# A decoder layer on one core: a new order for the start and the loop of its mixture of experts

## The chip, the core and the metric

The kernel runs on one core of a Trainium2 chip. A core has five engines that take instructions from queues of their own and meet only at semaphores: TensorE (PE in the profile, with PEld for its weight loads), VectorE (DVE), ScalarE (ACT), GpSimd (POOL) and SyncE (SP), which here only issues DMAs. Every queue is worked off in the order in which it was written; an instruction that waits holds up all that stand behind it on its engine.

The metric is the device time of one execution in microseconds (us), on one core. The changed kernel is compared with the kernel before by that.

## The reference

One decoder layer on x of 4 x 256 tokens by 256 features: 16 gated heads (projection, causal convolution, layer norm, a decaying state), an attention over a context, and a mixture of experts. The change is in the last, and where it begins:

```python
scores = sigmoid(hidden @ gate_weight.T)                  # 1024 tokens x 16 experts
choice = scores + bias                                    # 4 groups of 4 experts
# sum of the two best of each group -> keep 2 groups -> keep the 4 best experts of them
topk_weight = 2.5 * topk_weight / (topk_weight.sum(-1) + 1e-20)
g = einsum('th,nfh->ntf', hidden, gate_w)                 # 16 experts, 128 wide
u = einsum('th,nfh->ntf', hidden, up_w)
act = silu(g) * u
routed = einsum('ntf,nhf,tn->th', act, down_w, weight_matrix)
out = routed + swiglu(hidden, sh_gate_w, sh_up_w, sh_down_w)   # one shared expert, 256 wide
x = x + out
```

## The kernel before, in words

The program has three stages: the 16 heads in a software pipeline (up to about 400 us), a middle stage (last projection, layer norm, context attention, layer norm; about 400 to 430 us), and the experts. No scheduler places anything: each engine's order is the order of the code of its block, and semaphore counts tie the engines together.

The shared expert is cut into two of 128, so there are 18 experts, n = 1 to 18, of which 1 and 2 are the shared ones. The 1024 tokens are worked in NCH = 2 chunks c of N = 512. Each fp32 product is made of three fp32r products of a high and a low part (`mm3`, L1250 to L1254: low-high, high-low, high-high), so every matrix is first split: ACT copies the high part, POOL or DVE subtracts to get the low one. For one expert:

- SP loads its three weight matrices, 384 KB, into one half `s` of `w_raw` (`load_expert`, DMA L356).
- ACT and POOL split the two matrices of the first products (`gate_up_high` L759, `gate_up_low` L482) and that of the second (`down_high` L766, `down_low` L488) into the same half of `w_hi` and `w_lo`.
- PE makes g and u of each chunk into four banks, 24 matmuls of 512 columns (`gate_up`).
- ACT takes silu(g) (`gate_silu`, `tok`, L775), DVE multiplies by u (`u_times`, `conv`, L1142), POOL multiplies by the routing weights (`weigh`, `gate<-conv,tap`, L500), ACT and DVE split the product (`act_high` L784, `act_low` L1151, tiles `gated_hi` and `gated_lo`).
- PE makes the second product, 24 matmuls of 256 columns, added up in banks 4 to 7 (`down`).

Below, G(n) is `gate_up` of expert n on PE and D(n) its `down`. PE goes G(n+1), D(n). Buffers for silu, product and split product are single.

The routing weights of an expert are a row of `route_rows` in DRAM. SP loads it, spread over 128 partitions, 512 KB, into one half of `tap0` (`load_route`, DMA L378); `weigh(n)` waits for it. For experts 1 and 2 the weight is 1, made by a memset on POOL (L506). The rows come out of the routing chain: PE makes the logits (L1252 to L1254 with `wv_hi`), ACT the sigmoid, PE transposes to tokens (L1613), ACT copies (L804), DVE runs some 40 small dependent operations (L1171 to L1231), PE transposes back (L1628), ACT copies to `routeT` (L816), SP writes `route_rows` (L372). While that chain runs, the engines work on experts 1 to 3 in between.

Of the kernel before, what the change touches and what calls it, by code (L numbers as in the profile page):

```python
# [25 lines left out]
P = 128  # L26
# [4 lines left out]
N = 512  # L31
# [95 lines left out]
def decoder_layer(nc, x_in, ctx_in, xw_in, xb_in, wb_in, bb_in, w_in, prm_in, wv_in, wo_in,  # L127
# [5 lines left out]
    with ctx:  # L133
# [75 lines left out]
        act_w = gate  # L209
        act_hi, act_lo = gated_hi[:, 0:T], gated_lo[:, 0:T]  # L210
        wb_hi, wb_lo = act_hi[:, 0:KT * H], act_lo[:, 0:KT * H]

# [45 lines left out]
        ones_ready = sem("ones_ready")  # L258
# [9 lines left out]
        def _(sp):  # L268
# [90 lines left out]
            def expert_split(n):  # L359


                sp.wait_ge(down_lo_ready, n - E_SHARED)


# [5 lines left out]
            load_expert(4, 1)  # L370
            sp.wait_ge(r_tr_ready, NCH)
# [3 lines left out]
            def load_route(e, s, before):  # L375

                sp.wait_ge(e_weighted, before)
                sp.dma_start(wbc[:, s * T:(s + 1) * T],  # L378
                             route_rows[bass.ds(e, 1), :].broadcast_to([P, T])).then_inc(ld_route[s], 16)

            for s in range(2):
                load_route(s, s, NCH * (s + 1))
# [12 lines left out]
        def _(pool):  # L395
# [89 lines left out]
            def down_low(n, s):  # L485
                w = slice(s * 3 * D + 2 * D, (s + 1) * 3 * D)
                pool.wait_ge(down_hi_ready, n - E_SHARED)
# [3 lines left out]
            def weigh(n, s, first):  # L491

                for c in range(NCH):
                    pool.wait_ge(u_prod, (n - 1) * NCH + c + 1)
                    if not first:

                        pool.wait_ge(e_hi, (n - 2) * NCH + c + 1)
                        pool.wait_ge(e_lo, (n - 2) * NCH + c + 1)
                    cc = slice(c * N, (c + 1) * N)
                    nc.gpsimd.tensor_tensor(act_w[:, cc], prod[:, cc], wbc[:, s * T + c * N:s * T + (c + 1) * N],  # L500
                                            ALU.mult).then_inc(e_weighted, 1)
# [12 lines left out]
            def step(n, s, left=2):  # L514

                pool.wait_ge(ld_route[s], (n - 1 - s) * 8)
                weigh(n, s, False)
                if left > 1:
                    gate_up_low(n + 2, s)
                if left > 0:  # L520
                    down_low(n + 1, 1 - s)

            with pool.Fori(0, E_ROUTED // 2 - 1) as r:
                for s in range(2):
                    step(r * 2 + (3 + s), s)
            step(E_ALL - 1, 0, 1)
            step(E_ALL, 1, 0)
# [3 lines left out]
        def _(act):  # L531
# [220 lines left out]

            def gate_up_high(n, s):
# [3 lines left out]
                act.wait_ge(e_full, n * 4 - 8)  # L757
# [3 lines left out]
            def down_high(n, s):  # L761
                act.wait_ge(ld_w[s], n * 8 + (8 * (H - 1 - s) + 16))
# [5 lines left out]
            def gate_silu(n, first):  # L768

                for c in range(NCH):  # L770
                    act.wait_ge(e_full, (n - 1) * 4 + 2 * c + 1)
                    if not first:
                        act.wait_ge(u_prod, (n - 2) * NCH + c + 1)
                    cc = slice(c * N, (c + 1) * N)
                    nc.scalar.activation(silu_g[:, cc], e_ring[2 * c][:, :], ACT.Silu).then_inc(g_silu, 1)  # L775

            def act_high(n, first):

                for c in range(NCH):
                    act.wait_ge(e_weighted, (n - 1) * NCH + c + 1)  # L780
                    if not first:
                        act.wait_ge(e_down, n - 1)
                    cc = slice(c * N, (c + 1) * N)
                    nc.scalar.activation(act_hi[:, cc], act_w[:, cc], ACT.Copy).then_inc(e_hi, 1)  # L784
# [5 lines left out]
            context_soft(1)  # L790
            context_att()
# [5 lines left out]
            for c in range(NCH):  # L797

# [3 lines left out]

            act.wait_ge(r_tok_full, 1)
            nc.scalar.activation(score, bank[4][:, 0:TT * E_ROUTED], ACT.Copy).then_inc(r_tok_ready, 1)  # L804
            gate_silu(1, True)
            gate_up_high(3, 0)
            act_high(1, True)
            gate_silu(2, False)
            gate_up_high(4, 1)
            act_high(2, False)  # L810
            down_high(3, 0)

# [6 lines left out]
            def step(n, s, left=2):  # L819
                gate_silu(n, False)  # L820
                if left > 1:
                    gate_up_high(n + 2, s)
                act_high(n, False)
                if left > 0:
                    down_high(n + 1, 1 - s)

            with act.Fori(0, E_ROUTED // 2 - 1) as r:
                for s in range(2):
                    step(r * 2 + (3 + s), s)
# [872 lines left out]
```

## Time and profile before

| | us |
|---|---|
| median of 3 runs (lowest, highest) | 597.23 (596.89, 598.12) |
| the profiled execution's own time | 597.47 |
| its span in the profile | 595.7 |
| PE busy | 558.7 (94% of the span) |
| DVE busy | 433.7 (73%) |
| ACT busy | 399.5 (67%) |
| POOL busy | 299.0 (50%) |

The busy times are sums over the span; matmuls overlap by design, so a PE that is busy 10.00 of 10 us is one without a gap, and the distance between the starts of two matmuls is what one costs. The profile names a tile by what its buffer was first made for: in the experts' stage `tok` is silu(g), `conv` the product with u, `gate` the weighted product, `gated_hi` and `gated_lo` its two parts, `obet` and `raw` the routing's tiles, `tap` the weights of one expert.

### The profile page before, as it was taken

How to read it: one execution, taken by the hardware profiler on the slowest of the kernel's cores; microseconds unless marked ns; L12 is line 12 of the kernel's file. 1: busy time of each engine (PE TensorE's matmuls, PEld its weight loads, DVE VectorE, ACT ScalarE, POOL GpSimd, SP SyncE). 2: the span in 40 equal slices, each digit the busy share in tenths (PEclk: the TensorE clock that was granted, in tenths of full speed). 3: DMA queues.
4: the chain of work that ended last, by engine and by line, in shares of the span. 5: the costliest groups of instructions: out<-in, count | busy, mean ns of one | idle time of the engine just before them, and what ended most of it. 6: DMA issues, size and time to landing. Idle time of an engine off the chain costs nothing.

```text
span 595.7 us, 10301 instructions
## 1 busy us (share of the span) xinstructions
PE 558.7 (94%) x3392; PEld 490.0 (82%) x3392; DVE 433.7 (73%) x1018; ACT 399.5 (67%) x783; POOL 299.0 (50%) x201
## 2 busy tenths in 40 slices
PE   3899999999999999999999999896687999999996
PEld 1687899989989989989989989786475888888885
DVE  8778989889989988998998998955676433333334
ACT  4978988878978979879779778674442433344331
POOL 2434756746746646656656563301032755556542
PEclk9998999999999999999999999998797999999999
DMA  6122032032032032032031020110001523333311
GB/s 202 41 99 81 0 117 81 1 115 81 2 117 81 2 115 81 2 116 80 2 116 55 28 97 27 55 30 0 1 1 51 172 101 110 102 123 115 105 62 70
DMA packets 16267, 42.23 MB, mean 71 GB/s; under 512 B 4544, under 2 KB 4800, under 8 KB 16224
## 3 DMA queue, kind: packets, MB, share of 16 engines
q1 hardware_dynamic: 16224, 41.69, 21.1%
q8 instruction: 23, 0.38, 0.3%
q14 instruction: 20, 0.16, 0.1%
HBM read 40.47 MB, written 1.21 MB: 70 GB/s over the span
## 4 chain that ended last, share of the span: by engine, by line
PE 84%; DVE 8%; ACT 5%; issue 1%; DMA 1%; SPq 0%; DVEq 0%; ACTq 0%
PE bank L1252 20%; PE bank L1254 19%; PE bank L1253 19%; PE bank L1248 15%; PE bank L1386 4%; PE bank L1374 4%; ACT tok L622 2%; PE bank L1263 1%; DMA xbias<-in_xb 1%; DVE stats L969 1%; ACT values L536 1%; DVE stats L889 1%; DVE x L1242 0%; DVE raw L988 0%; DVE conv L1142 0%
## 5 line engine op out<-in xcount | busy, mean ns | idle before, releaser
L1252 PE MATMUL bank<-xT_lo,w_hi 128*128 128x512 f32 x336 | 140.7, 419 | 2.3 <-DVE conv L988 1.2
L1254 PE MATMUL bank<-xT_hi,w_hi 128*128 128x512 f32 x336 | 132.6, 395 | 0.0
L1253 PE MATMUL bank<-xT_hi,w_lo 128*128 128x512 f32 x336 | 132.4, 394 | 0.0
L423 POOL TENSOR_TENSOR gated_lo<-gated,gated_hi 128x512 fp32r<-128x512 f32 x30 | 38.7, 1289 | 116.5 <-ACT gated_hi L642 112.8
L622 ACT ACTIVATE tok<-bank,nmr,rstd 128x128 f32<-128x128 f32 x256 | 91.2, 504 | 2.1 <-DVE nmr L884 2.1
L500 POOL TENSOR_TENSOR gate<-conv,tap 128x512 f32<-128x512 f32 x36 | 46.5, 1293 | 86.7 <-DVE conv L1142 76.0
L1252 PEld LDWEIGHTS bank<-xT_lo,w_hi 128*128 128x128 f32 x336 | 63.9, 190 | 17.4 <-DVE conv L988 3.2
L1254 PEld LDWEIGHTS bank<-xT_hi,w_hi 128*128 128x128 f32 x336 | 63.6, 189 | 14.4
L418 POOL TENSOR_TENSOR conv<-tap,conv 128x506 f32<-128x506 f32 x32 | 61.9, 1934 | 21.7 <-DVE conv L988 21.7
L418 POOL TENSOR_TENSOR raw<-tap,raw 128x506 f32<-128x506 f32 x32 | 62.0, 1936 | 20.4 <-DVE raw L988 16.3
L1253 PEld LDWEIGHTS bank<-xT_hi,w_lo 128*128 128x128 f32 x336 | 64.1, 191 | 9.7
L969 DVE BATCH_NORM_STATS2 stats<-bank 128x6 f32<-128x128 f32 x256 | 56.4, 284 | 16.1 <-PE bank L1374 16.1
L960 DVE TENSOR_TENSOR_SCAN decay<-obet,dmask 128x1536 f32<-128x1536 f32 x16 | 62.0, 3872 | 0.0
L1142 DVE TENSOR_TENSOR conv<-bank,tok 128x512 f32<-128x512 f32 x36 | 24.9, 691 | 46.1 <-PE bank L1254 43.8
L1151 DVE TENSOR_TENSOR gated_lo<-gate,gated_hi 128x512 fp32r<-128x512 f32 x36 | 25.4, 746 | 44.1 <-ACT gated_hi L784 44.1
L634 ACT ACTIVATE qk<-bank,prm 128x512 f32<-128x512 f32 x64 | 51.3, 841 | 0.0
L988 DVE SCALAR_TENSOR_TENSOR raw<-bank,prm,raw 128x510 f32<-128x510 f32 x64 | 46.8, 743 | 5.6 <-ACT tap L590 4.5
L1248 PE MATMUL bank<-qk 128*128 128x256 f32 (+1 forms) x256 | 50.2, 329 | 0.5 <-DVE x L1021 0.3
L988 DVE SCALAR_TENSOR_TENSOR conv<-bank,prm,conv 128x510 f32<-128x510 f32 x64 | 46.8, 743 | 3.4 <-ACT tap L590 2.2
L1248 PEld LDWEIGHTS bank<-qk 128*128 128x128 f32 x256 | 43.2, 190 | 5.6 <-issue 0.7
L1248 PE MATMUL bank<-probs,values 128*128 128x256 f32 (+1 forms) x256 | 46.9, 327 | 0.0
L784 ACT ACTIVATE gated_hi<-gate 128x512 fp32r<-128x512 f32 x36 | 21.0, 625 | 37.6 <-PE bank L1254 32.4
(167 smaller groups left out, 1374.3 us busy)
## 6 DMA issues: line engine op xcount, KB each, us to landing
w_raw<-in_w SPq DMA_DIRECT2D x34, 384.0 KB, 4.4
obet<-obet_rows SPq DMA_DIRECT2D x16, 768.0 KB, 4.3
tap<-route_rows SPq DMA_DIRECT2D x16, 512.0 KB, 3.6
wv_raw<-in_wv SPq DMA_DIRECT2D x8, 256.0 KB, 4.9
wo_raw<-in_wo SPq DMA_DIRECT2D x8, 256.0 KB, 5.0
x<-in_x SPq DMA_DIRECT2D x2, 512.0 KB, 4.7
out_x<-x SPq DMA_DIRECT2D x4, 256.0 KB, 2.4
raw<-in_ctx SPq DMA_DIRECT2D x1, 512.0 KB, 5.4
```

The source lines that it names most:

```text
L418: nc.gpsimd.tensor_tensor(y, r, y, ALU.add).then_inc(conv_done, 1)
L423: nc.gpsimd.tensor_tensor(gated_lo[:, cc], gated[:, c * N:(c + 1) * N], gated_hi[:, cc].bitcast(F32), ALU.subtract).then_inc(gated_lo_read ...
L500: nc.gpsimd.tensor_tensor(act_w[:, cc], prod[:, cc], wbc[:, s * T + c * N:s * T + (c + 1) * N], ALU.mult).then_inc(e_weighted, 1)
L622: ins = nc.scalar.activation(tok[:, t * P:(t + 1) * P], t_ring[u][:, i * P:(i + 1) * P], ACT.Identity, scale=rstd[:, t:t + 1], bias=nmr[:, ...
L634: nc.scalar.activation(qk[:, u * N:(u + 1) * N], t_ring[u][:, :], ACT.Identity, scale=prm[:, o:o + 1], bias=prm[:, o + 1:o + 2]).then_inc( ...
L960: nc.vector.tensor_tensor_scan(decay[:, :], obet[:, :], dmask[:, :], 0.0, ALU.mult, ALU.add).then_inc(decay_ready, 1)
L969: ins = nc.vector.bn_stats(stats[:, 6 * t:6 * t + 6], t_ring[u][:, i * P:(i + 1) * P])
L988: ins = nc.vector.scalar_tensor_tensor(out=y, in0=r, scalar=prm[:, o + 3 - back:o + 4 - back], in1=y, op0=ALU.mult, op1=ALU.add)
L1248: return nc.tensor.matmul(o, l, r, start=start, stop=stop)
L1252: nc.tensor.matmul(o, l_hi, r_lo, start=start, stop=False, skip_group_check=loose)
L1253: nc.tensor.matmul(o, l_lo, r_hi, start=False, stop=False, skip_group_check=loose)
L1254: return nc.tensor.matmul(o, l_hi, r_hi, start=False, stop=stop, skip_group_check=loose)
```

## The change

The middle stage keeps its order but for two pieces put into it. From there on:

- PE's loop goes G(n), D(n-2) in place of G(n), D(n-1): the first products are two experts ahead. Silu, product, weighted product and its two parts get two buffers each.
- Experts 3 and 4 are split as a whole in the middle stage, into `wv_hi`/`wv_lo` and `wo_hi`/`wo_lo`, which the heads have left (`early_high` on ACT, one piece before `context_att`; `early_low` on POOL after the first addition of `x`). SP loads experts 5 and 6 at once behind them.
- POOL does nothing between that and the end of the routing chain: experts 1 and 2 are no longer weighed, their product is split directly, the memset is gone, and the splits of 5 and 6 wait for `r_ready`.
- In the routing chain DVE takes the first product of expert 1 before it and `act_low` of expert 2 into it; PE transposes to tokens after one bank of G(1) in place of two, and makes all of G(3) and half of D(2) before it waits for the routing weights, where it made half of G(3).
- In the loop POOL goes `weigh` of chunk 0, `gate_up_low(n+1)`, `weigh` of chunk 1, `down_low(n)`. SP goes `load_route(n)`, wait for `down_low(n)`, `load_expert(n+2)`.

The diff at its core:

```diff
@@ sync
+            for n in (5, 6):
+                sp.wait_ge(w_lo_ready, n - 2 + H)
+                load_expert(n, 1 - n % 2)
...
-            def load_route(e, s, before):
-                sp.wait_ge(e_weighted, before)
+            def load_route(e, s):
+                if not (isinstance(e, int) and e < 2):
+                    sp.wait_ge(e_weighted, e * NCH - NCH)
...
-            with sp.Fori(0, E_ROUTED // 2 - 1) as r:
+            with sp.Fori(0, E_ROUTED // 2 - 2) as r:
                 for s in range(2):
-                    expert_split(r * 2 + (3 + s))
-                    load_expert(r * 2 + (5 + s), s)
-                    load_route(r * 2 + (2 + s), s, r * (2 * NCH) + NCH * (3 + s))
+                    load_route(r * 2 + (2 + s), s)
+                    sp.wait_ge(down_lo_ready, r * 2 + (s + 1))
+                    load_expert(r * 2 + (7 + s), s)
+            for s in range(2):
+                load_route(E_ROUTED - 2 + s, s)
@@ gpsimd
-            pool.wait_ge(p_added, TT // 2)
-            nc.gpsimd.memset(wbc, 1.0).then_inc(ones_ready, 1)
-            pool.wait_ge(ones_ready, 1)
-            weigh(1, 0, True)
-            gate_up_low(3, 0)
-            weigh(2, 1, False)
-            gate_up_low(4, 1)
-            down_low(3, 0)
+            pool.wait_ge(x_mixed, 1)
+            early_low(3)
+            early_low(4)
+            pool.wait_ge(r_ready, 1)
+            gate_up_low(5, 0)
+            gate_up_low(6, 1)
...
+            def step(n, m, s, up=True, down=True):
+                pool.wait_ge(ld_route[s], n * 8 - (1 + s) * 8)
+                weigh(n, m, s, 0)
+                if up:
+                    gate_up_low(n + 1, 1 - s)
+                weigh(n, m, s, 1)
+                if down:
+                    down_low(n, s)
@@ scalar
+            def step(n, m, s, up=True):
+                gate_silu(n, m)
+                if up:
+                    gate_up_high(n + 1, 1 - s)
+                act_high(n, m)
+                down_high(n, s)
@@ vector
+            u_times(1, 1, (0,))
             dve.wait_ge(r_tok_ready, 1)
...
-            u_times(1, True, (0,))
...
-            act_low(1)
-            u_times(2, chunks=(0,))
+            u_times(2, 2, (0,))
+            act_low(1, 1)
...
+            act_low(2, 2)
             op(nc.vector.tensor_tensor(weight, same, score, ALU.mult))
@@ tensor
-            gate_up(1, 0, True, (0,))
+            gate_up(1, 0, ((0, 0),))
...
-            down(1, 0, True, False)
-            gate_up(3, 0, chunks=(0,))
+            down(1, 1, 0)
+            gate_up(3, 0)
+            down(2, 2, 1, (0,))
             pe.wait_ge(r_ready, 1)
...
-            with pe.Fori(0, E_ROUTED // 2 - 1) as r:
+            with pe.Fori(0, E_ROUTED // 2 - 2) as r:
                 for s in range(2):
-                    gate_up(r * 2 + (5 + s), s)
-                    down(r * 2 + (4 + s), 1 - s, False, False)
-            down(E_ALL, 1, False, True)
+                    gate_up(r * 2 + (7 + s), s)
+                    down(r * 2 + (5 + s), 5 + s, s)
+            down(E_ALL - 1, E_ALL - 1, 0)
+            down(E_ALL, E_ALL, 1)
```

SyncE from the write of `route_rows` through its loop, in the kernel before (`tap0` is the routing weights of one expert, L356 the load of an expert's weights):

```order
L372 DMA route_rows<-gate 16x1024 [waits r_tr_ready]
L378 DMA tap0<-route_rows 128x1024 [waits e_weighted,ld_route_rows]
L378 DMA tap0<-route_rows 128x1024 [waits e_weighted]
...
L356 ISA [waits down_lo_ready]
L356 DMA w_raw<-in_w 128x768
...
L378 ISA [waits e_weighted]
L378 DMA tap0<-route_rows 128x1024
```

The same place now (L390 loads the routing weights, L370 an expert's weights):

```order
L390 DMA tap0<-route_rows 128x1024 [waits ld_route_rows]
L390 DMA tap0<-route_rows 128x1024
...
L390 ISA [waits e_weighted]
L390 DMA tap0<-route_rows 128x1024
...
L370 ISA [waits down_lo_ready]
L370 DMA w_raw<-in_w 128x768
...
L390 ISA [waits e_weighted]
L390 DMA tap0<-route_rows 128x1024
```

In both, the load of a row of routing weights stands behind a load of expert weights and that load's wait for a `down_low`. Before, the row of expert n stood behind `down_low(n-2)`; now it stands behind `down_low(n-1)`.

GpSimd in one half of its loop, in the kernel before:

```order
L494 ISA [waits ld_route1]
L500 TENSOR_TENSOR gate<-conv,tap0 128x512 [waits e_lo,e_hi,u_prod]
...
L500 TENSOR_TENSOR gate<-conv,tap0 128x512 [waits e_lo,e_hi,u_prod]
...
L482 TENSOR_TENSOR w_lo<-w_raw,w_hi 128x512 [waits w_hi_ready]
L488 TENSOR_TENSOR w_lo<-w_raw,w_hi 128x256 [waits down_hi_ready]
```

And now:

```order
L515 ISA [waits ld_route1]
...
L520 TENSOR_TENSOR gate<-conv,tap0 128x512 [waits e_lo,e_hi]
...
L497 TENSOR_TENSOR w_lo<-w_raw,w_hi 128x512 [waits w_hi_ready]
...
L520 TENSOR_TENSOR gate<-conv,tap0 128x512 [waits e_lo,e_hi]
...
L503 TENSOR_TENSOR w_lo<-w_raw,w_hi 128x256 [waits down_hi_ready]
```

The split of the next first weights moved between the two weighings; the split of the down weights, which before was that of expert n+1, is now that of expert n and stands behind both.

## Rows read from the trace of the kernel before

**Rows 1.** Windows: stretch, length, busy us of the five, PEclk, DMA share, GB/s.

```profile
440.00:450.00 10.00, 8.46 (x49) 6.93 (x47) 9.72 (x23) 2.92 (x6) 5.27 (x5) 1.00 0.00 0
450.00:460.00 10.00, 5.81 (x20) 3.99 (x19) 5.19 (x11) 3.03 (x6) 1.76 (x2) 0.66 0.10 29
460.00:480.00 20.00, 20.00 (x124) 17.98 (x123) 8.05 (x9) 6.95 (x13) 12.51 (x11) 1.00 0.46 154
```

**Rows 2.** Timeline of PE in routing: start, us, instruction, [idle before <- its releaser].

```profile
444.30 0.36 PE L1252 MATMUL bank<-w_lo,gated_hi 128*128 128x256 f32 x1 [1.54 <-DVE gated_lo L1151]
...
453.59 1.88 PE L1628 MATMUL bank<-ident,obet 128*16 128x128 f32 x8 [3.52 <-DVE obet L1231]
456.14 0.79 PE L1252 MATMUL bank<-xT_lo,w_hi 128*128 128x512 f32 x1 [0.68 <-ACT gate L816]
...
460.46 0.28 PE L1252 MATMUL bank<-w_lo,gated_hi 128*128 128x256 f32 x1
```

**Rows 3.** Timeline of DVE in the routing chain.

```profile
434.68 0.29 DVE L1171 TENSOR_TENSOR obet<-obet 128x128 f32<-128x128 f32 x1 [5.28 <-ACT obet L804]
...
437.82 1.27 DVE L1195 TENSOR_TENSOR raw<-raw,tie 128x128 f32<-128x128 f32 x1
439.13 0.29 DVE L1196 TENSOR_TENSOR raw<-raw 128x128 f32<-128x128 f32 x1
...
443.46 1.29 DVE L1151 TENSOR_TENSOR gated_lo<-gate,gated_hi 128x512 fp32r<-128x512 f32 x2
...
451.22 0.69 DVE L1223 TENSOR_TENSOR raw<-raw 128x128 f32<-128x128 f32 x1
```

**Rows 4.** Timeline of POOL in the same stretch.

```profile
437.53 1.41 POOL L500 TENSOR_TENSOR gate<-conv,tap 128x512 f32<-128x512 f32 x1 [32.82 <-DVE conv L1142]
...
462.47 2.54 POOL L500 TENSOR_TENSOR gate<-conv,tap 128x512 f32<-128x512 f32 x2 [10.71 <-DMA tap<-route_rows]
```

**Rows 5.** Timeline of SP: its DMA issues.

```profile
458.05 0.81 SPq L378 DMA_DIRECT2D tap<-route_rows  x2
459.22 0.35 SPq L356 DMA_DIRECT2D w_raw<-in_w  x1
...
482.79 0.33 SPq L356 DMA_DIRECT2D w_raw<-in_w  x1
```

**Rows 6.** DMA issues from 450 us, KB, median to landing; under it L378's spread.

```profile
w_raw<-in_w SPq DMA_DIRECT2D x14, 384.0 KB, 3.0
...
DMA to landing us min/median/max: 3.3/3.6/5.0
```

**Rows 7.** POOL in the loop; the last row gives min/median/max ns of L488.

```profile
468.84 2.54 POOL L500 TENSOR_TENSOR gate<-conv,tap 128x512 f32<-128x512 f32 x2 [1.23 <-DVE conv L1142]
...
481.60 1.02 POOL L488 TENSOR_TENSOR w_lo<-w_raw,w_hi 128x256 fp32r<-128x256 f32 x1 [0.77 <-ACT w_hi L766]
...
L488 POOL TENSOR_TENSOR w_lo<-w_raw,w_hi x16: 748/1016/1088, 451.0 to 580.9; 128x256 fp32r<-128x256 f32 x16
```

**Rows 8.** Timeline of ACT late in the loop.

```profile
579.35 1.16 ACT L784 ACTIVATE gated_hi<-gate 128x512 fp32r<-128x512 f32 x2 [3.63 <-PE bank L1254]
580.41 0.40 ACT L766 ACTIVATE w_hi<-w_raw 128x256 fp32r<-128x256 f32 x1
```

**Rows 9.** Timeline of PE: starts of G(5), D(4), G(6); then the end of the stage.

```profile
471.53 0.40 PE L1252 MATMUL bank<-xT_lo,w_hi 128*128 128x512 f32 x1
...
477.01 0.28 PE L1252 MATMUL bank<-w_lo,gated_hi 128*128 128x256 f32 x1
...
479.81 0.40 PE L1252 MATMUL bank<-xT_lo,w_hi 128*128 128x512 f32 x1
...
589.12 0.36 PE L1252 MATMUL bank<-w_lo,gated_hi 128*128 128x256 f32 x1 [1.59 <-DVE gated_lo L1151]
...
591.88 0.27 PE L1254 MATMUL bank<-w_hi,gated_hi 128*128 128x256 f32 x1
```

**Rows 10.** Timeline of ACT in the middle stage, behind `context_att`.

```profile
406.68 2.07 ACT L536 ACTIVATE values<-x,nmr,rstd 128x256 f32<-128x256 f32 x4 [2.37 <-DVE nmr L884]
```

More of the change, by code:

```diff
@@ L486, in down_low @@
                 w = slice(s * 3 * D + 2 * D, (s + 1) * 3 * D)
-                pool.wait_ge(down_hi_ready, n - E_SHARED)
+                pool.wait_ge(down_hi_ready, n - 4)
                 nc.gpsimd.tensor_tensor(w_lo[:, w], w_raw[:, w], w_hi[:, w].bitcast(F32),
                                         ALU.subtract).then_inc(down_lo_ready, 1)
[L491 to L501, printed above, removed]
@@ L523, in _, with early_low, weigh @@
-            with pool.Fori(0, E_ROUTED // 2 - 1) as r:
+            def early_low(n):
+                hi, lo = early(n)
+                s = 1 - n % 2
+                pool.wait_ge(w_hi_ready, n + H)
+                nc.gpsimd.tensor_tensor(lo, w_raw[:, s * 3 * D:(s + 1) * 3 * D], hi.bitcast(F32),
+                                        ALU.subtract).then_inc(w_lo_ready, 1)
+            def weigh(n, m, s, c):
+                pool.wait_ge(u_prod, n * NCH + (c + 1 - NCH))
+                if not (isinstance(n, int) and n < 5):
+                    pool.wait_ge(e_hi, n * NCH + (c + 1 - 3 * NCH))
+                    pool.wait_ge(e_lo, n * NCH + (c + 1 - 3 * NCH))
+                nc.gpsimd.tensor_tensor(weighted(m, c), prod[:, two(m, c)],
+                                        wbc[:, s * T + c * N:s * T + (c + 1) * N],
+                                        ALU.mult).then_inc(e_weighted, 1)
@@ L766, in down_high, with gate_silu, act_high @@
                 nc.scalar.activation(w_hi[:, w], w_raw[:, w], ACT.Copy).then_inc(down_hi_ready, 1)
[L768 to L784, printed above, removed]
+            def gate_silu(n, m, chunks=range(NCH)):
+                for c in chunks:
+                    act.wait_ge(e_full, n * 4 + (2 * c - 3))
+                    if not (isinstance(n, int) and n < 3):
+                        act.wait_ge(u_prod, n * NCH + (c + 1 - 3 * NCH))
+                    nc.scalar.activation(silu_g[:, two(m, c)], e_ring[2 * c][:, :], ACT.Silu).then_inc(g_silu, 1)
+            def act_high(n, m, chunks=range(NCH)):
+                for c in chunks:
+                    if m <= E_SHARED:
+                        act.wait_ge(u_prod, (n - 1) * NCH + c + 1)
+                    else:
+                        act.wait_ge(e_weighted, n * NCH + (c + 1 - 3 * NCH))
+                        act.wait_ge(e_down, n - 2)
+                    nc.scalar.activation(act_hi[:, two(m, c)], weighted(m, c), ACT.Copy).then_inc(e_hi, 1)
             act.wait_ge(ld["router"], 32)
@@ L790, in _ @@
             context_soft(1)
+            early_high(3)
+            early_high(4)
             context_att()
@@ L796, in _, with router_scores @@
                     half_out(i, c, dst)
-            for c in range(NCH):
+            def router_scores(c):
                 act.wait_ge(r_full, c + 1)
@@ L817, in _ @@
                                      ACT.Copy).then_inc(r_tr_ready, 1)
[L819 to L827, printed above, removed]
+            def step(n, m, s, up=True):
[4 more added lines that the diff above has]
+                down_high(n, s)
+            gate_silu(4, 4)
+            act_high(3, 3)
+            gate_silu(5, 5)
+            act_high(4, 4)
+            act_high(5, 5)
+            down_high(5, 0)
+            step(6, 6, 1)
+            with act.Fori(0, E_ROUTED // 2 - 3) as r:
                 for s in range(2):
-                    step(r * 2 + (3 + s), s)
-            step(E_ALL - 1, 0, 1)
-            step(E_ALL, 1, 0)
+                    step(r * 2 + (7 + s), 7 + s, s)
+            step(E_ALL - 1, E_ALL - 1, 0)
+            step(E_ALL, E_ALL, 1, False)
         @block.vector
@@ L1587, in down @@
[L1587 to L1602 removed]
+                hi, lo = w_hi[:, s * 3 * D:(s + 1) * 3 * D], w_lo[:, s * 3 * D:(s + 1) * 3 * D]
@@ new lines, in gate_up @@
+                if isinstance(n, int) and n in (3, 4):
+                    hi, lo = early(n)
+                for c, j in parts:
+                    if not (isinstance(n, int) and n == 1):
+                        pe.wait_ge(g_silu if j == 0 else u_prod, n * NCH + (c + 1 - 2 * NCH))
+                    for kt in range(KT):
+                        o = j * D + kt * P
+                        ins = mm3(e_ring[2 * c + j][:, :], hi[:, o:o + P], lo[:, o:o + P],
+                                  xs_(xT_hi, kt, c * N, (c + 1) * N), xs_(xT_lo, kt, c * N, (c + 1) * N),
+                                  kt == 0, kt == KT - 1)
+                    ins.then_inc(e_full, 1)
```

170 lines of the change are left out of this document (97 added, 73 removed).

## The prediction, made before the changed kernel ran

> **What bounds the kernel now.** I read the windows first, to see where PE has gaps. From 460 us on PE is busy 20.00 of 20 us at full clock; between 440 and 460 it is busy 8.46 and 5.81 of 10 [rows 1]. So the experts' loop is bound by PE itself, and only its start has something to give. The timeline of PE gives the loop's beat: G(5) starts at 471.53, D(4) at 477.01, G(6) at 479.81, so a G is 5.48, a D 2.80, together 8.28 us [rows 9]. At that beat no other engine's order can make the loop faster, but a chain longer than 8.28 us per expert can make it slower. The gaps are these: 1.54 us before D(1), 3.52 before the routing transposes, 0.68 before the second half of G(3), and 1.59 before D(18) [rows 2, 9]. Then the timeline of DVE, since the 3.52 end with its chain, and those of SP and POOL, since their order in the loop is what the change turns.
>
> **What the start gains.** The clock: with the 3.52 us gap the mean granted clock of 450 to 460 is 0.66, and with the 1.54 gap that of 440 to 450 stays 1.00 [rows 1, 2]. The second half of G(3) takes 4.32 us (456.14 to 460.46) against 2.74 at full clock, the eight transposes 1.88 [rows 2], of which I take half, 0.94, as clock.
>
> DVE's chain runs from 434.68 to 453.5 without a pause [rows 2, 3]. Seven of its small operations, from the first at 437.82 (1.27 us) to the last at 451.22 (0.69), lie beside a POOL instruction such as that of 437.53 and cost 7.8 us, where the same shape takes 0.29 [rows 3, 4]: some 5.9 us. With POOL idle they go. The chain starts 0.4 later (first product of expert 1 ahead of it), loses 0.8 (that product and a wait inside it) and gets `act_low(2)`, 1.2 net of overlap [rows 3]. It ends at 453.5 + 0.4 - 5.9 - 0.8 + 1.2 = 448.4. By then PE has G(3) and half of D(2) ahead of it: G(2) ends at 442.6, and D(1) needs `act_low(1)`, which now stands behind no weighing and is due at about 442.0. So D(1) runs to 445.4, G(3) to 450.9, half of D(2) to 452.3, and the transposes find the weights ready. All three gaps and the low clock go: 1.54 + 3.52 + 0.68 + 1.58 + 0.94 = 8.3 us. G(4) starts at 455.0, not 463.3 (460.46 + 2.80). At the end D(17) and D(18) both follow G(18), and 1.6 us goes too. With the old beat in between that would be 9.9 us.
>
> **What the middle stage pays.** Two ACT copies before `context_att`: behind it ACT waits 2.37 us for the norm [rows 10], and two copies of 768 columns are shorter than that, with 0.53 for 512 [rows 8]. I take 0. Two subtractions on POOL beside DVE's additions and statistics of `x`: no row shows these beside a POOL instruction that reads SBUF. Bounds: 0, and 1.0 for one DVE operation held as at 437.82 [rows 3]; I take 0, since DVE waits there for PE's sums one after the other and has room. The Trainium skill, page "SBUF — State Buffer", section "SBUF: two separate sides", says that DVE and GpSimd exclude each other only where DVE has two SBUF inputs or a two-port mode. By it the statistics (one input) and the additions (one input in PSUM) go free; the rows of the routing chain, all from SBUF, agree with its other half.
>
> **What the loop pays.** This decides. In SP's queue the load of row n stands behind the load of expert n+1, which waits for `down_low(n-1)`. POOL's step n begins with `weigh(n)`, which waits for row n, and ends with `down_low(n)`. So POOL waits for SP, and SP for POOL's last instruction, one full turn per expert with a whole DMA in it. The buffer has been free for long; the place in the queue alone makes the chain. One turn:
>
> - `down_low(n-1)` ends to SP's issue: 481.60 + 1.02 to 482.79, 0.17 [rows 5, 7].
> - The load of expert n+1 is issued ahead: 0.45, from two issues in 0.81 [rows 5].
> - Row n lands. Alone 3.3 to 5.0, median 3.6; the 5.0 had another row's load right in front [rows 6]. Here 384 KB stand in front, alone 3.0 [rows 6]. In the one burst of the trace (two rows and an expert from 458.05) POOL had its first row at 462.47, after 4.4 [rows 4, 5]. I take 4.3; bounds 3.6 and 5.0. Then 0.05 to POOL.
> - Three POOL operations (weigh, low part of the next first weights, weigh) by 2.54 for two: 3.8 [rows 7]. The low part's source has landed before the row.
> - `act_high` of chunk 1 and `down_high` on ACT, 0.53 + 0.40 and hand-overs: 1.03 [rows 8].
> - `down_low(n)`: 1.02, the median; bounds 0.75 and 1.09 [rows 7].
> - POOL's second weighing beside DVE's `act_low` of chunk 0: 0 to 0.34 (1.09 - 0.75) [rows 7], I take 0.17; and 0.1 for SP's loop branch every second turn, an estimate, bounds 0 and 0.2.
>
> Sum: 0.17 + 0.45 + 4.35 + 3.8 + 1.03 + 1.02 + 0.27 = 11.1 us, against PE's 8.28. Low bound 9.8, high 12.1. G(n+1) waits for its low part, the second of the three POOL operations, so PE takes this beat and stands idle 2.8 us before each G.
>
> The Trainium skill, page "DMA: Bandwidth & Descriptors", section "Anatomy of one DMA", gives about 2.0 us fixed plus bytes at 436 GB/s for a DMA issued from GpSimd. Put here, as an estimate, 896 KB would land 4.1 us after the first issue, so 3.65 after the row's, and a turn would be 10.4. This trace is above it: 3.0 for 384 KB, where it gives 2.9, and 3.6 for a row, where it gives 3.2.
>
> Where the turns begin: PE has made its transposes at 453.2 (with ACT's copies about 454.1). From ACT's copy to the first weighing it was 6.33 us (456.14 to 462.47) [rows 2, 4], so `weigh(3)` starts at 460.4 and ends at 462.9. Row 5 is issued then and lands at 466.8 (3.6 + 0.2, nothing before it). `weigh(5)`, ACT and `down_low(5)` take 2.54 + 1.03 + 1.02: 471.4. Then expert 7 and row 6: 0.17 + 0.45 + 4.35, 476.35. G(7) starts two POOL operations later, 478.95. PE has done G(4) to G(6), D(3), D(4) by 455.0 + 16.4 + 5.6 = 477.0 and waits 1.9. From G(7) to G(18) are 11 turns: 478.95 + 122.1 = 601.05. After G(18) stand D(16), D(17), D(18), with the work of expert 18 (some 4 us) under the first two: 5.48 + 8.40 + 0.16 for the last matmul's end = 14.04, so 615.1. The old kernel's PE ended at 592.15 and its span at 595.7: 3.55 more [rows 9]. Span 618.6. The profiled execution is 1.77 above its span and 0.24 above the median of the runs, so the time is 618.6 + 1.77 - 0.24 = 620.2 us, 23 slower.
>
> **The rivals.**
>
> *The loop stays at PE's beat.* Then the 9.9 us are won: 587.3. For it: PE has a lead of two experts, and before POOL's wait for the first row [rows 4] was its only one on a row. Against: a lead of any length is used up by a turn that is longer than the beat, and for a turn of 8.28 row n would have to land 1.5 us after its issue; the fastest took 3.3 [rows 6]. It needs that I read the queue wrongly. 5%.
>
> *Cheaper turns.* The row lands as if alone, 3.6, and nothing collides: 9.8, so 11 x 1.3 = 14.3 less, 606. 15%.
>
> *Dearer turns.* Row at 5.0 and collisions: 12.1, 631. 12%.
>
> *The clock falls in the waits.* A wait of 2.8 lies between the 1.54 that cost nothing and the 3.52 that did [rows 1, 2]. G would be slower by 1.6 per half at the low clock [rows 2]. Up to 2.8 a turn this hides in PE's wait, since POOL's turn doesn't see it; only after the last wait it counts: 2 to 3 us, 623, inside my range. PE could become the bound at up to (5.48 + 2.80) x 2 only if the clock never came back, and in every busy stretch it did. 10% for a cost that shows.
>
> **How the numbers follow.** The forecast, turns near 11, has 58%, the rivals 5, 15, 12 and 10. All but the first are slower. A measurement of this kernel tells 0.2% (1.2 us) from no change. Faster 5%, same 1%, slower 94%. The range of 8 in 10 goes from 608 to 630; it leaves out the first rival and the outer halves of the two on the turns.
>
> **What would show it.** Right: PE waits 2 to 3 us before each G from G(7) on, released by POOL's low part; the largest wait of POOL is on the load of `tap`, about 4.5 us each, 12 or 13 times; each `tap` issue lies 0.4 to 0.5 behind a `w_raw` issue; G starts 10 to 12 us apart; the routing stage without its gaps, G(4) starting near 455, DVE's small operations all near 0.3. Wrong: `tap` issued well before `down_low`, or G's 8.28 apart. If the turns are right and the total isn't, the start's 8.3 is the term to look at.

## The result, and the profile after

The kernel after takes 630.69 us (median of 4 runs, 626.80 to 633.84) against 597.06 us (596.17 to 598.12) for the kernel before on the same chip: a ratio of 1.0559, 95% interval 1.0489 to 1.0630. The prediction was 620.2 us, with a range of 608 to 630. The kernel is slower, as forecast, and in the place that was forecast, but its time lies 10.5 us above the forecast and 0.7 us above the upper end of the range. The profiled execution took 628.59 us, its span is 626.6.

The windows show both halves of the change. Columns are as in [rows 1]: the stretch, its length, busy us of PE, PEld, DVE, ACT and POOL, granted clock, DMA share, GB/s.

```profile
440.00:450.00 10.00, 10.00 (x61) 8.78 (x60) 7.44 (x28) 3.38 (x6) 0.98 (x1) 1.00 0.00 0
450.00:460.00 10.00, 10.00 (x57) 8.48 (x56) 1.38 (x2) 2.26 (x4) 1.73 (x3) 1.00 0.33 106
460.00:470.00 10.00, 10.00 (x58) 8.74 (x57) 7.69 (x8) 4.86 (x9) 9.06 (x6) 1.00 0.16 60
470.00:480.00 10.00, 6.47 (x37) 5.67 (x36) 3.10 (x4) 2.57 (x5) 4.97 (x4) 0.88 0.28 93
480.00:500.00 20.00, 18.45 (x94) 15.59 (x92) 5.15 (x7) 5.94 (x11) 6.21 (x6) 0.89 0.28 93
500.00:600.00 100.00, 75.94 (x392) 64.68 (x393) 26.85 (x34) 28.44 (x52) 45.19 (x36) 0.93 0.22 73
```

PE is busy 10.00 of 10 us through the whole routing stage, where it was busy 8.46 and 5.81 [rows 1]. Then, from 470 us, it has gaps: in the loop it is busy 75.94 of 100 us, where it had none (80.00 of 80 us from 500 to 580 in the kernel before).

The routing chain on DVE has become what was forecast. The shape that took 1.27 us beside GpSimd [rows 3] takes 0.28 to 0.29 in the whole chain (`L1244` is the old L1195):

```profile
435.55 0.29 DVE L1244 TENSOR_TENSOR raw<-raw,tie 128x128 f32<-128x128 f32 x1
...
446.27 0.29 DVE L1281 TENSOR_TENSOR obet<-obet 128x128 f32<-128x128 f32 x1
```

The loss stands in the timeline of SyncE. First comes each expert's weights, then the row of routing weights, and both wait for the last instruction of GpSimd's step:

```profile
506.73 0.33 SPq L370 DMA_DIRECT2D w_raw<-in_w  x1
507.63 0.33 SPq L390 DMA_DIRECT2D tap<-route_rows  x1
519.07 0.33 SPq L370 DMA_DIRECT2D w_raw<-in_w  x1
519.69 0.33 SPq L390 DMA_DIRECT2D tap<-route_rows  x1
```

And in the timeline of POOL beside it (the bracket is the idle time before, and what ended it):

```profile
505.62 0.94 POOL L503 TENSOR_TENSOR w_lo<-w_raw,w_hi 128x256 fp32r<-128x256 f32 x1 [1.05 <-ACT w_hi L803]
512.75 1.26 POOL L520 TENSOR_TENSOR gate<-conv,tap 128x512 f32<-128x512 f32 x1 [6.19 <-DMA tap<-route_rows]
513.97 1.26 POOL L497 TENSOR_TENSOR w_lo<-w_raw,w_hi 128x512 fp32r<-128x512 f32 x1
515.19 1.72 POOL L520 TENSOR_TENSOR gate<-conv,tap 128x512 f32<-128x512 f32 x1
517.96 0.93 POOL L503 TENSOR_TENSOR w_lo<-w_raw,w_hi 128x256 fp32r<-128x256 f32 x1 [1.05 <-ACT w_hi L803]
```

Read one turn through both: `down_low` ends at 506.56, the weights are issued at 506.73, the row at 507.63; the row releases the weighing at 512.75; `down_low` ends at 518.89, and the next issue is at 519.07. That is 12.3 us for an expert, and a load is in it from issue to landing. The timeline of PE shows that it takes this turn as its own (start of G(7), G(8), G(9), G(10), then G(18)):

```profile
478.60 0.79 PE L1309 MATMUL bank<-xT_lo,w_hi 128*128 128x512 f32 x1 [3.52 <-POOL w_lo L497]
...
491.44 0.49 PE L1309 MATMUL bank<-xT_lo,w_hi 128*128 128x512 f32 x1 [1.54 <-POOL w_lo L497]
...
503.01 0.49 PE L1309 MATMUL bank<-xT_lo,w_hi 128*128 128x512 f32 x1 [3.01 <-POOL w_lo L497]
...
515.37 0.79 PE L1309 MATMUL bank<-xT_lo,w_hi 128*128 128x512 f32 x1 [3.83 <-POOL w_lo L497]
...
608.73 0.49 PE L1309 MATMUL bank<-xT_lo,w_hi 128*128 128x512 f32 x1 [1.67 <-POOL w_lo L497]
```

From 478.60 to 608.73 there are 11 turns of 11.83 us, against PE's 8.28 before [rows 9]. The waits from 455 us on, summed (engine, line, releaser: us, times, longest), name the same chain: GpSimd waits for the row, ScalarE for GpSimd, and PE for the low part of its weights:

```profile
POOL gate L520 <- DMA tap<-route_rows: 71.1, 13, 8.3
ACT gated_hi L821 <- POOL gate L520: 64.0, 27, 3.5
...
PE bank L1309 <- POOL w_lo L497: 30.8, 12, 3.8
```

### The profile page after: what moved, and what is told of

The parts are those of the page before. It is cut to its first block, busy times and chain, and to the rows that moved or that the text cites. A ratio compares the mean times of both kernels' runs of the same rounds, so it can differ in the third digit from the quotient of the medians.

```text
span 626.6 us, 10166 instructions
## 1 busy us (share of the span) xinstructions
PE 567.1 (91%) x3392; PEld 495.0 (79%) x3392; DVE 434.0 (69%) x1018; ACT 400.5 (64%) x781; POOL 295.9 (47%) x194
## 4 chain that ended last, share of the span: by engine, by line
PE 64%; issue 8%; POOL 8%; DMA 7%; DVE 5%; ACT 5%; SPq 1%; POOLq 0%; DVEq 0%; ACTq 0%
PE bank L1305 14%; PE bank L1309 14%; PE bank L1311 13%; PE bank L1310 13%; DMA tap<-route_rows 7%; PE bank L1443 4%; PE bank L1431 4%; POOL gate L520 4%; POOL w_lo L497 3%; ACT tok L645 2%; POOL w_lo L503 1%; PE bank L1320 1%; DMA w_raw<-in_w 1%; DVE stats L1017 1%; ACT values L559 1%
## 5 line engine op out<-in xcount | busy, mean ns | idle before, releaser
L1309 PE MATMUL bank<-xT_lo,w_hi 128*128 128x512 f32 x320 | 138.2, 432 | 32.4 <-POOL w_lo L497 30.8
L1311 PE MATMUL bank<-xT_hi,w_hi 128*128 128x512 f32 x320 | 128.9, 403 | 0.0
L1310 PE MATMUL bank<-xT_hi,w_lo 128*128 128x512 f32 x320 | 128.3, 401 | 0.0
L1309 PEld LDWEIGHTS bank<-xT_lo,w_hi 128*128 128x128 f32 x320 | 62.5, 195 | 49.3 <-issue 33.1
L1200 DVE TENSOR_TENSOR gated_lo<-gate,gated_hi 128x512 fp32r<-128x512 f32 x32 | 29.5, 925 | 74.5 <-ACT gated_hi L821 74.5
L1311 PEld LDWEIGHTS bank<-xT_hi,w_hi 128*128 128x128 f32 x320 | 62.0, 194 | 14.4
L1310 PEld LDWEIGHTS bank<-xT_hi,w_lo 128*128 128x128 f32 x320 | 62.8, 196 | 9.9
```

The lines of the kernel that those rows point to most:

```text
L1309: nc.tensor.matmul(o, l_hi, r_lo, start=start, stop=False, skip_group_check=loose)
L1310: nc.tensor.matmul(o, l_lo, r_hi, start=False, stop=False, skip_group_check=loose)
L1311: return nc.tensor.matmul(o, l_hi, r_hi, start=False, stop=stop, skip_group_check=loose)
```

## The experiments

The theory: the place of the row's load in SyncE's queue makes a serial turn of SyncE, DMA, GpSimd and ScalarE, and nothing else of the change costs time. The rivals: the new order of GpSimd's step costs it, or the new order of PE, or the weights' landing. And within the theory one question was open, since the prediction's turn was too short: what makes the row's landing long. Nine kernels were run; each ratio is to the kernel before on the same chip, with its 95% interval.

### The row early

Only SyncE changes: the load of a row stands one expert earlier, ahead of the wait for `down_low`.

```diff
-            for s in range(2):
-                load_route(s, s)
+            for s in range(4):
+                load_route(s, s % 2)
             with sp.Fori(0, E_ROUTED // 2 - 2) as r:
                 for s in range(2):
-                    load_route(r * 2 + (2 + s), s)
+                    load_route(r * 2 + (4 + s), s)
                     sp.wait_ge(down_lo_ready, r * 2 + (s + 1))
                     load_expert(r * 2 + (7 + s), s)
-            for s in range(2):
-                load_route(E_ROUTED - 2 + s, s)
```

> The changed kernel with one edit in SyncE's order: the row of routing weights of expert n is loaded ahead of the wait for down_low(n-2), and no longer behind down_low(n-1). All DMAs and all other queues stay. Theory A (the turn POOL - SP - row - POOL sets the loop): the turn is cut, since the row is issued a whole step before it is needed; PE takes its own beat of 8.28 us again, no waits before G(7) to G(18), time about 587 us, ratio to the kernel before 0.983. Rival B (the load of the expert's weights, which still stands behind down_low, is what the loop waits for): POOL no longer waits for tap, but PE still waits before each G, starts of G 11 to 12 us apart, time over 620. In between: the weights' own turn (end of D(n-2), act_high, down_high, down_low, DMA 3.0, gate_up_high, gate_up_low) is 7.9 us by the rows of before against 8.28; should it be a little over, 0.5 us a step, about 593.

Measured: 596.86 us (594.99 to 599.32), ratio 0.9997 (0.9981 to 1.0014). The place of one load is worth 34 us, so the turn is shown. But it came out 10 us above what I expected: the gains of the start are there, and something in the loop eats them. The timeline of POOL (here L495 is the low part of the next first weights):

```profile
494.02 1.29 POOL L518 TENSOR_TENSOR gate<-conv,tap 128x512 f32<-128x512 f32 x1 [1.28 <-DVE conv L1190]
497.18 1.29 POOL L495 TENSOR_TENSOR w_lo<-w_raw,w_hi 128x512 fp32r<-128x512 f32 x1 [1.87 <-ACT w_hi L795]
...
500.77 0.93 POOL L501 TENSOR_TENSOR w_lo<-w_raw,w_hi 128x256 fp32r<-128x256 f32 x1 [1.05 <-ACT w_hi L801]
502.78 1.29 POOL L518 TENSOR_TENSOR gate<-conv,tap 128x512 f32<-128x512 f32 x1 [1.08 <-DVE conv L1190]
506.17 1.28 POOL L495 TENSOR_TENSOR w_lo<-w_raw,w_hi 128x512 fp32r<-128x512 f32 x1 [2.10 <-ACT w_hi L795]
```

No weighing of the loop waits for a row any more (the two such waits that are left, 8.7 us, stand ahead of it). From 497.18 to 506.17 is a second turn, 8.99 us: the low part of expert n+1, the second weighing, ACT, `down_low(n)`, and only then SyncE may load the weights of n+2 (issued at 501.88), whose high part GpSimd then awaits. It too is longer than 8.28, by 0.7 us. From G(7) to G(18) a turn is 9.04 us in the mean, 8.4 us more in 11 turns than at PE's beat, and PE waits another 2.04 us before G(7).

### The row behind `down_low`, but ahead of the weights

```diff
                     sp.wait_ge(down_lo_ready, r * 2 + (s + 1))
+                    load_route(r * 2 + (3 + s), 1 - s)
                     load_expert(r * 2 + (7 + s), s)
```

> The changed kernel, where row n is still issued only behind down_low(n-1), but ahead of the load of expert n+1's weights and not behind it. The turn stays closed, the row has nothing in front. Theory A: the turn loses the 0.74 us between the two issues and the row lands in 3.5 and not 4.7: 11.75 - 0.74 - 1.2 = 9.8 us a turn, 11 turns, about 21 us less than the changed kernel: 609. Rival B (weights): now the weights land later, so the time is the same or up to 5 us longer, 630 to 635.

Measured: 618.12 us (617.62 to 618.49), ratio 1.0351 (1.0332 to 1.0370). The turn is 10.86 (row issues from 480.74 to 589.29, ten turns). It lost the spacing of the two issues, but the row, from its issue to the weighing, became shorter only from 4.70 to 4.27 us, not to 3.5, with nothing in front of it and 384 KB 0.52 us behind it:

```profile
480.74 0.33 SPq L390 DMA_DIRECT2D tap<-route_rows  x1
481.26 0.33 SPq L370 DMA_DIRECT2D w_raw<-in_w  x1
```

### GpSimd's order turned back

```diff
                 weigh(n, m, s, 0)
+                weigh(n, m, s, 1)
                 if up:
                     gate_up_low(n + 1, 1 - s)
-                weigh(n, m, s, 1)
```

> The changed kernel with only POOL's order in a step turned: both weighings, then gate_up_low(n+1), then down_low(n). The same instructions. Theory A: gate_up_low (1.25 us) fills POOL's wait of 1.05 for ACT's act_high and down_high, so a turn is about 1.0 us shorter: 10.7, 11 turns, 11 less, about 619, though each G now starts behind three POOL operations and not two. Rival B: G waits for gate_up_low, which now comes 1.3 us later in every step, so the time is longer, 640 to 645.

Measured: 626.96 us (622.71 to 628.25), ratio 1.0509 (1.0482 to 1.0536): 3.7 us better than the kernel after, though the executions of the two overlap (622.71 to 628.25 and 626.80 to 633.84). So the new order of GpSimd is no main cause, and turning it back is not worth the 11 us that theory A gave it. The turn is 11.1 us in the mean (issues of weights from 470.59 to 592.76, eleven turns). ACT's 1 us hides beside the low part in some turns, but in others a weighing waits for its product, since G of that expert started a GpSimd operation later:

```profile
510.16 1.30 POOL L520 TENSOR_TENSOR gate<-conv,tap 128x512 f32<-128x512 f32 x1 [6.10 <-DMA tap<-route_rows]
512.60 1.29 POOL L520 TENSOR_TENSOR gate<-conv,tap 128x512 f32<-128x512 f32 x1 [1.14 <-DVE conv L1192]
```

### PE one ahead again, the row early

The kernel of the first experiment, and PE's loop back to G(n), D(n-1).

```diff
+            down(5, 5, 0)
...
                     gate_up(r * 2 + (7 + s), s)
-                    down(r * 2 + (5 + s), 5 + s, s)
-            down(E_ALL - 1, E_ALL - 1, 0)
+                    down(r * 2 + (6 + s), 6 + s, 1 - s)
             down(E_ALL, E_ALL, 1)
```

> The edit of e1_row_early, and PE's loop back to G(n), D(n-1), with D(4) and D(5) behind G(6); the rest of the change stays. It prices the first products two ahead once the rows come in time. If PE is the bound in both, this differs only at the end, by the gap before D(18) of 1.6 us: 588.6. If the two-ahead order itself is what is short of time for the weights in e1_row_early, this one is faster than that.

Measured: 601.99 us (599.84 to 602.61), ratio 1.0074 (1.0046 to 1.0101), 5 us slower than with two ahead. So PE's new order costs nothing; it wins.

### The weights in two loads

The row early, and an expert's weights in two DMAs: the 256 KB of the first product as soon as their half has been split, the 128 KB of the second behind `down_low`. That takes the second turn away as well.

```diff
+            def load_up(n, s):
+                sp.wait_ge(w_lo_ready, n + (H - 2))
+                ... # columns 0 to 2 * D, counts on ld_w[s]
+            def load_down(n, s):
+                sp.wait_ge(down_lo_ready, n - 6)
+                ... # columns 2 * D to 3 * D, counts on ld_d[s]
...
-                    load_route(r * 2 + (2 + s), s)
-                    sp.wait_ge(down_lo_ready, r * 2 + (s + 1))
-                    load_expert(r * 2 + (7 + s), s)
+                    load_up(r * 2 + (7 + s), s)
+                    load_route(r * 2 + (4 + s), s)
+                    load_down(r * 2 + (7 + s), s)
@@ down_high
+                    act.wait_ge(ld_d[s], n * 8 - (40 + 8 * s))
```

> Both turns opened. Rows are loaded ahead as in e1_row_early; from expert 7 on the weights come in two DMAs: the two matrices of the first products (256 KB) right behind gate_up_low(n-2), a step earlier than now, and the down matrix (128 KB) behind down_low(n-2) as before. Compute queues as in the changed kernel, but for ACT's down_high, which waits for its own load. Theory A2: e1_row_early still had a second turn, 8.97 us a step: gate_up_low(n+1) - weigh(n, chunk 1) - act_high - down_high - down_low(n) - DMA of n+2 - gate_up_high(n+2) - gate_up_low(n+2). With it open PE is without a wait from G(1) to D(18) and steps at 8.28: 0.7 x 11 = 7.6 less than e1_row_early's 596.9, less the first wait of 2.0 and its low clock of 1.7: about 586, ratio 0.982. Rival: the steps of 8.97 come from PE's or the memory's contention and not from that turn: then the time stays at 597.

Measured: 587.30 us (586.49 to 588.30), ratio 0.9838 (0.9820 to 0.9857). It beats both kernels. The windows have no gap left:

```profile
440.00:450.00 10.00, 10.00 (x57) 8.66 (x56) 8.91 (x31) 2.67 (x5) 0.00 (x0) 1.00 0.00 0
450.00:460.00 10.00, 10.00 (x60) 8.61 (x59) 1.38 (x2) 3.90 (x7) 2.52 (x2) 1.00 0.29 92
460.00:480.00 20.00, 20.00 (x112) 17.50 (x111) 11.73 (x13) 8.56 (x16) 15.04 (x11) 1.00 0.43 148
480.00:580.00 100.00, 100.00 (x595) 88.78 (x594) 32.11 (x48) 36.84 (x70) 56.97 (x47) 1.00 0.29 93
```

In the timeline of PE, the starts of G(4), G(7) and G(8):

```profile
454.90 0.39 PE L1320 MATMUL bank<-xT_lo,wo_hi 128*128 128x512 f32 x1
...
477.15 0.39 PE L1320 MATMUL bank<-xT_lo,w_hi 128*128 128x512 f32 x1
485.41 0.40 PE L1320 MATMUL bank<-xT_lo,w_hi 128*128 128x512 f32 x1
```

### The weights in two loads, PE one ahead

The same, with the change of PE's loop shown above.

> e5_split_loads with PE's loop back to G(n), D(n-1). It prices the two-ahead order alone. Theory: PE is the bound in both, so the lead is worth only the gap before D(18), 1.6 us and a little clock: 587.5 to 588. Rival: the lead also covers waits in the loop, so this is 3 us or more behind e5_split_loads.

Measured: 590.30 us (588.97 to 590.72), ratio 0.9881 (0.9862 to 0.9900). Two ahead is worth 3 us here, and all of it lies before and in D(18). PE has no other wait from 440 us on than the one before D(18), so the rival with waits in the loop falls, though its 3 us came true. The timeline shows the gap that I expected, and the windows behind it more than the little clock that I had allowed for, half the full one: D(18) takes 4.14 us from its first start to its last (580.46 to 584.60), where it took 2.76 [rows 9]. 1.79 and 1.38 make 3.2:

```profile
580.46 0.39 PE L1320 MATMUL bank<-w_lo,gated_hi 128*128 128x256 f32 x1 [1.79 <-POOL w_lo L513]
```

```profile
580.00:582.00 2.00, 1.54 (x11) 1.54 (x12) 0.53 (x1) 0.00 (x0) 0.41 (x1) 0.90 0.00 0
582.00:584.00 2.00, 2.00 (x12) 2.00 (x11) 1.08 (x3) 0.00 (x0) 0.00 (x0) 0.50 0.35 131
```

### The weights in two loads, GpSimd busy in routing

Nine multiplications of 512 columns on GpSimd from 432.06 to 443.3, into tiles that nobody reads: what is the idle GpSimd worth?

```diff
+            pool.wait_ge(r_tok_ready, 1)
+            for scratch in (decay, probs, qk):
+                for i in range(3):
+                    nc.gpsimd.tensor_tensor(scratch[:, i * N:(i + 1) * N], attT[:, 0:N], attT[:, N:2 * N],
+                                            ALU.mult)
             pool.wait_ge(r_ready, 1)
```

> e5_split_loads with nine more multiplications of 128x512 on POOL, from r_tok_ready on, into tiles that nobody reads any more (some 11.3 us of POOL, beside DVE's routing chain). The output doesn't depend on them. Theory: POOL's instructions that read SBUF hold DVE's small ones up by about 1 us each, as in the kernel before, so that the chain ends 6 to 9 us later; 3.9 us of that lie under PE's lead, the rest is a gap on PE: 2 to 5 us, more with the clock, time 589 to 592. Rival: DVE's long operations in the kernel before had another cause: no difference to e5_split_loads, DVE's small operations at 0.29.

Measured: 596.27 us (594.72 to 598.95), ratio 0.9993 (0.9977 to 1.0008): 9 us slower than without them, where I expected 2 to 5. The timeline of DVE, and what PE waits for:

```profile
435.89 1.32 DVE L1244 TENSOR_TENSOR obet<-obet 128x32 f32<-128x32 f32 x1
437.13 1.32 DVE L1245 TENSOR_TENSOR obet<-obet 128x32 f32<-128x32 f32 x1
...
443.60 0.19 DVE L1251 TENSOR_TENSOR obet<-obet 128x32 f32<-128x32 f32 x1
```

```profile
446.28 0.79 PE L1325 MATMUL bank<-xT_lo,w_hi 128*128 128x512 f32 x1 [6.63 <-DVE conv L1208]
```

Seven operations of this shape, these two among them, stand from 434.77 to 442.04 and take 1.17 to 1.32 us each, while 0.19 is what the shape takes once GpSimd is done. The miss is that I had looked at the chain's end. The second product of expert 1 (445.54) stands in DVE's queue behind these operations, and PE waits for it, 6.63 us, long before it needs the routing weights. Behind the wait the clock is lower: 0.61 in the mean of 447 to 452, which costs 2.0 us more (5 x 0.39). The Trainium skill, page "SBUF — State Buffer", section "SBUF: two separate sides", calls the port pair of DVE and GpSimd an exclusive lock held for a whole instruction. These rows agree: each small operation lasts as long as one multiplication on GpSimd.

### The row late, the weights in two loads

The row again behind `down_low(n-1)`, but only 128 KB in front of it, and 256 KB behind it; no weights can be late.

```diff
                     load_route(r * 2 + (2 + s), s)
-                    sp.wait_ge(down_lo_ready, r * 2 + (s + 1))
-                    load_expert(r * 2 + (7 + s), s)
+                    load_up(r * 2 + (7 + s), s)
+                    load_down(r * 2 + (7 + s), s)
```

> The split loads of e5_split_loads, so that no G waits for its weights, but row n stands again behind the wait for down_low(n-1), now with only 128 KB in front of it. Theory A: the first turn is closed again and sets the loop: 0.17 + 0.6 + 4.0 (less in front than 384 KB) + 5.2 + 0.93 = 10.9 a turn, 11 turns, 621. Rival B (what cost the time was the weights): about 587, as e5_split_loads.

Measured: 625.35 us (624.47 to 627.78), ratio 1.0490 (1.0464 to 1.0516). So the row's turn alone makes the loss, without any help of the weights: 38 us against the same kernel with the row early. From a row's issue to the weighing that waited for it it is 4.39 us in the mean of 11 rows; one more weighing waited for its product.

### The row late and alone

The weights in two loads and the row behind `down_low(n-1)` once more, but in front of all weights, and SyncE waits for the row's landing before it issues any.

```diff
+                    sp.wait_ge(down_lo_ready, r * 2 + (s + 1))
+                    load_route(r * 2 + (3 + s), 1 - s)
+                    landed(r * 2 + (3 + s), 1 - s)
+                    load_down(r * 2 + (7 + s), s)
+                    load_up(r * 2 + (8 + s), 1 - s)
```

> The weights of an expert are loaded in two DMAs, and the row of expert n stands behind down_low(n-1) as in the kernel after, but alone in flight: SyncE issues the next weights only once the row has landed. Theory A: the row took 4.7 us in the kernel after because of the DMAs ahead of it and behind it in the same queue. Alone it lands in 3.6 us, a turn is 0.17 + 3.6 + 0.05 + 5.2 + 0.93 = 9.95 us, and 11 turns against 11 of 11.83 take 20 us off the profiled 626.6: about 606 to 611 us, with little spread between executions. Theory B: a row issued inside the loop lands in 4.3 to 4.7 us whatever is in flight beside it. Then a turn is 10.6 to 11 us and the time about 614 to 620 us. If the weights, now issued later, become the bound, gate_up_low waits for their landing and PE's waits name the DMA.

Measured: 612.06 us (610.05 to 612.82), ratio 1.0237 (1.0208 to 1.0265). It falls between the two, 1 us above the first theory's range and 2 below the second's. The timeline of SyncE shows the row alone (L378 and L372 load the weights):

```profile
504.42 0.33 SPq L403 DMA_DIRECT2D tap<-route_rows  x1
508.38 0.33 SPq L378 DMA_DIRECT2D w_raw<-in_w  x1
508.91 0.33 SPq L372 DMA_DIRECT2D w_raw<-in_w  x1
514.97 0.33 SPq L403 DMA_DIRECT2D tap<-route_rows  x1
```

From a row's issue to the weighing it is 3.92 us in the mean of 12 turns (3.53 to 4.15), and G starts every 10.25 us (480.31 to 593.07, eleven turns). Put together, for the rows issued inside the loop, with the landing of the DMA (median, lowest and highest) and the mean time from the row's issue to GpSimd's weighing:

| what is in flight beside the row | landing, us | row to weighing, us | turn, us | median time, us |
|---|---|---|---|---|
| 384 KB in front (kernel after) | 4.4 (3.7 to 5.3) | 4.70 | 11.83 | 630.69 |
| 128 KB in front, 256 KB behind | 4.2 (3.6 to 4.7) | 4.39 | 11.4 | 625.35 |
| 384 KB behind | 4.0 (3.7 to 4.7) | 4.27 | 10.86 | 618.12 |
| nothing | 3.7 (3.5 to 3.8) | 3.92 | 10.25 | 612.06 |
| row early, not in the turn | - | - | 8.27 | 587.30 |

The second line and the last two also have an expert's weights in two loads. Of the 1.58 us between the kernel after and the row alone, 0.76 are the issue of the weights that went out first, and 0.78 the row: neighbours in the same queue cost it up to 0.8 us. And the landings decide between the two theories, which the median time did not. Alone, a row inside the loop lands in 3.5 to 3.8 us, as the 3.6 of [rows 6]; that is the first theory. Its turn of 9.95 us was too short because it gave 0.05 us to the way from the landing to the weighing, and that way takes 0.25.

## Why the prediction was right in kind and wrong in size

**What the start gains: right.** G(4) was due at 455.0. In the kernel after it starts at 452.66, 2.3 us earlier, but 1.9 us of that had been won long before the change (see below). The windows of 25 to 50 us, first of the kernel after, then of that with two loads, differ in the clock (PEclk 1.00 and 0.93), and the kernel before has the 0.93 too:

```profile
25.00:50.00 25.00, 21.59 (x135) 18.43 (x135) 19.75 (x50) 20.43 (x41) 11.52 (x8) 1.00 0.23 74
```

```profile
25.00:50.00 25.00, 21.57 (x128) 18.36 (x127) 19.76 (x50) 20.25 (x40) 11.39 (x8) 0.93 0.23 74
```

The kernel with two loads has the same start of the experts, and it has G(4) at 454.90. Its median of 587.30 is also what the rival "The loop stays at PE's beat" gave: start and end are worth 9.7 us (596.96 to 587.30 on one chip), forecast 9.9. The gain needed another queue order and the weights in two loads.

**What the middle stage pays: right, nothing.** ACT's norm still waits 2.02 us behind the two copies, where it waited 2.37 [rows 10], and in the kernel with two loads it starts at 406.40, against 406.68 with the same early clock.

**The turn: the failed step.** Place, links and number of turns held; its size did not. Forecast 11.1, measured 11.83 from G(7) to G(18) (11.75 between SyncE's issues, of which the terms below are means):

| term of the turn | predicted | measured |
|---|---|---|
| `down_low` to SyncE | 0.17 | 0.17 |
| weights' issue to row's issue, loop branch | 0.55 | 0.76 |
| row's issue to weighing | 4.35 | 4.69 |
| weighing to `down_low`, with collision | 5.00 | 5.19 |
| `down_low` | 1.02 | 0.94 |

Three terms were each too small, and a turn repeated 11 times makes 8.0 us of 0.73.

- The spacing: the issues stand 0.62 apart inside the loop's body and 0.90 over its branch. The 0.45 came from two issues that stood in line [rows 5], and the 0.1 for the branch from no row; it measured 0.28 every second turn, 0.14 in the mean.
- The row: its landing was nearly right, 4.3 forecast and 4.4 in the mean (3.7 to 5.3). Too small was the way from the landing to the weighing, put at 0.05, which no run shows, where it takes 0.28 in the mean. The burst of [rows 4, 5] has it too: the first row landed 4.1 us after its issue and the weighing began after 4.4, which I read as a landing.
- The collision: the second weighing takes 1.72 us beside DVE's `act_low` in most turns, 0.46 over the first, where I took 0.17 from a bound made of other operations.

**From G(7) and to the end.** G(7) starts at 478.60 (forecast 478.95). That is luck, two errors that cancel: the execution was ahead by 1.9 us (its norm in the middle stage starts at 404.80, that of [rows 10] at 406.68), and the write of `route_rows` took 3.8 us where it had taken 1.9. From G(18) to the end it is 622.78 + 0.28 - 608.73 = 14.33, forecast 14.04. So the span's miss is 8.0 - 0.35 + 0.29 = 7.9, of 8.0 in all.

**From span to median.** Here 2.5 us more were lost. The profiled execution is 1.99 above its span (forecast 1.77), and the median 2.1 above it, where I carried over -0.24 from the kernel before. The executions of the kernel after lie 7 us apart, those of before 2. Eleven rows in series, each 3.9 to 5.6 from issue to weighing, would spread a time like that, and the early clock can add 1.9; no other execution of this kernel was profiled, so how much is each stays open.

**The clock.** It fell in the waits, as the rival said: the G behind the longest waits begin with matmuls of 0.79 us (478.60, 515.37), and 500 to 600 has 0.93. And it stayed hidden, as argued: GpSimd waited for its row in all but one turn of the loop, at 546.92, where the product was later.

**The range.** The dearer turn was in it, at 12.1 and 631, with 12%, but the range stopped at 630. The three terms all erred to one side: the spacing and the collision were taken from rows where the thing stood in other company, and the way from the landing to the weighing from no row.

## What to carry to other kernels

For each load, write down which wait stands in front of it in its queue, even a wait for something else: a load whose buffer is long free but that is queued behind the last instruction of its own consumer becomes a chain with a whole DMA in it, here 34 us for the place of one load. Look for the next turn before you expect the full gain from taking away the first: the second one, 9.0 us against 8.28, ate all that the start had won, and splitting one load by who reads it took it away. Where a turn repeats, take each of its terms from a row with the same company, and add the doubt of each to the range as many times as the turn runs.

## What the runs showed of the hardware that was not expected

- A 512 KB row landed in 3.5 to 3.8 us alone in its queue, and in 3.7 to 5.3 with 384 KB issued 0.6 to 0.9 us ahead; its reader started 0.25 to 0.28 us later in the mean. The Trainium skill, page "DMA: Bandwidth & Descriptors", section "Anatomy of one DMA", gives 2.0 us plus bytes at 436 GB/s for issue from GpSimd, by which 3.2 would be the estimate for this size. The rows here were issued from SyncE, and all landed later than that, the fastest in 3.3 us [rows 6].
- Work put behind a load slows it as well: with 384 KB issued 0.52 us behind it the row landed in 4.0 us in the median, against 3.7 alone.
- Not only operations with two inputs in SBUF were held beside GpSimd. In the kernel before, DVE's `tensor_scalar` of 440.91 (128x32) took 1.17 us and that of 448.68 (128x128) 1.22, each beside a weighing; in the kernel after the same two take 0.18 and 0.23.
- The gap of 1.79 us before D(18), with PE one ahead, was followed by a stretch at 0.50, that is 1.2 GHz; the gap of 1.59 at the same place in the kernel before was not [rows 9]. One execution of each was profiled.
- Two things changed from one profiled execution to another in code that was the same: the granted clock of 25 to 50 us, 0.93 to 1.00 over eleven kernels, and the write of 64 KB to `route_rows`, 1.9 to 3.8 us. Where that clock was 1.00, in five of the executions, the norm in the middle stage starts at 404.80 to 405.05; where it was 0.93 to 0.95, in six, at 406.15 to 406.77.
